# A node tile's steps in six places instead of eight, in a graph layer with a mixture of experts

## What is computed

```python
xn = layernorm(x)
# graph part: weighted sum over the edges of each node
n_emb = segment_sum(edge_weight[:, None] * xn[src], dst, 12500)
g = leaky(xn @ W1.T + b1 + (n_emb + n_emb * xn) @ W2.T + b2)
g = g / max(sqrt(sum(g * g)), 1e-12)
# mix part: linear attention; k and v are normalized per head, k.T @ v is a 32 x 32 table per head
ret = per_head(q(xn) @ (k(xn).T @ v(xn)) / 12500) + xn
m = gelu(ret @ w1 + b1) @ w2 + b2 + xn
x = x + g + m
# top-1 mixture of experts, 8 experts, each takes the first 1.25 * 12500 / 8 tokens
h = layernorm(x)
probs = softmax(h @ gate_w + gate_b); e = argmax(probs)
y = (relu(h @ w1[e] + b1[e]) @ w2[e] + b2[e]) * probs[e] * kept
return x + y
```

## Time and profile before

| What | Value |
|---|---|
| median of three runs | 2520.43 us |
| the profiled execution | 2522.2 us, its span 2520.3 us |
| mean granted clock of TensorE | 0.919 of full speed |
| busy: PE, DVE, ACT, POOL | 82%, 60%, 41%, 72% of the span |
| moved by DMA | 594.32 MB, mean 236 GB/s |
| POOL's last gather of edge rows | 2213.83 us |

### The profile page before, as it was taken

How to read it: one execution, slowest core, us unless ns; L and a number is a source line. 1 busy time by engine, 2 the same in 40 slices (tenths; PEclk the granted TensorE clock), 3 DMA queues, 4 the chain that set the end, 5 groups by cost and what they waited for, 6 DMA issues and landing times. The chain is left out here.

```text
span 2520.3 us, 42814 instructions
## 1 busy us (share of the span) xinstructions
PE 2056.2 (82%) x12889; PEld 1586.9 (63%) x12889; DVE 1514.9 (60%) x5328; ACT 1036.6 (41%) x2482; POOL 1810.3 (72%) x1888
## 2 busy tenths in 40 slices
PE   0049999994677777899989999998989899796898
PEld 0015656662455556776767777777777777685787
DVE  6676555554457786787646656666556556555233
ACT  4662333331344454553434433443444444342333
POOL 7777777777777777777777777777777777723654
PEclk9968999997788888999989999999999999897999
DMA  9845666664566667777777776777888888775896
GB/s 338 310 142 169 175 173 175 174 174 131 153 197 193 193 198 259 231 240 231 237 229 248 239 229 221 241 236 237 320 280 306 300 316 285 247 260 221 330 349 248
DMA packets 279341, 594.32 MB, mean 236 GB/s; under 512 B 48437, under 2 KB 177214, under 8 KB 256863
## 3 DMA queue, kind: packets, MB, share of 16 engines
q0 software_dynamic: 93168, 256.28, 33.8%
q1 hardware_dynamic: 155553, 284.06, 32.6%
q10 hardware_dynamic: 30390, 51.21, 5.5%
HBM read 506.22 MB, written 87.99 MB: 236 GB/s over the span
## 5 line engine op out<-in xcount | busy, mean ns | idle before, releaser
L931 POOL DMA_INDIRECT rows_sb<-xn_scratch,src_sb x1517 | 1459.0, 962 | 464.2 <-issue 455.8
L1199 PE MATMUL bank<-acc 128*128 128x128 f32 (+1 forms) x2624 | 442.3, 322 | 15.0 <-issue 10.9
L1220 PE MATMUL bank<-acc 128*128 128x256 f32 x1680 | 413.1, 390 | 0.0
L1199 PEld LDWEIGHTS bank<-acc 128*128 128x128 f32 x2624 | 384.9, 204 | 40.8 <-issue 18.6
L1020 PE MATMUL bank<-rows_sb,s_sb 128*24 128x256 f32 x3082 | 225.7, 413 | 202.0 <-DMA rows_sb<-xn_scratch,src_sb 197.4
L1963 ACT ACTIVATE acc<-bank,acc 128x128 f32<-128x128 f32 (+1 forms) x656 | 212.0, 398 | 375.8 <-PE bank L1199 375.7
L1220 PEld LDWEIGHTS bank<-acc 128*128 128x128 f32 x1680 | 313.9, 194 | 49.7 <-issue 0.9
L1484 DVE TENSOR_TENSOR acc<-acc,bank 128x48 f32 x831 | 170.4, 205 | 273.7 <-PE bank L1030 160.4
L1020 PEld LDWEIGHTS bank<-rows_sb,s_sb 128*24 128x24 f32 x3082 | 84.9, 107 | 274.9 <-issue 232.5
L1884 ACT COPY sums<-bank 120x256 f32<-120x256 f32 x208 | 76.5, 368 | 347.2 <-PE bank L1020 347.2
L1915 ACT ACT_TABLE_LOAD x95 | 121.9, 1283 | 194.8 <-PE bank L1109 193.9
(11 more groups left out here) (263 smaller groups left out, 3649.9 us busy)
## 6 DMA issues: line engine op xcount, KB each, us to landing
acc<-ffn_first_in SPq DMA_DIRECT2D x82, 1028.0 KB
acc<-ffn_w_in SPq DMA_DIRECT2D x82, 1024.0 KB
arena<-xn_scratch SPq DMA_DIRECT2D x194, 128.0 KB, 3.2
h_scratch<-arena ACTq DMA_DIRECT2D x97, 256.0 KB
rows_sb<-xn_scratch,src_sb POOLq DMA_INDIRECT x1517
xnt_scratch<-arena SPq DMA_DIRECT2D x97, 128.0 KB, 2.3
arena<-xnt_scratch SPq DMA_DIRECT2D x97, 128.0 KB
arena<-x_in SPq DMA_DIRECT2D x97, 128.0 KB
```

Source lines behind the costliest of these rows:

```text
L931: pool.indirect_dma_start(out=chunk_row(c), out_offset=None, in_=xn_d, in_offset=bass.IndirectOffsetOnAxis(ap=src_sb[:, c:c + 1], axis=0)) ...
L1199: m = pe.matmul(bank[:, i * tokens:(i + 1) * tokens], w1_sb[k % 2][:, h, f * P:(f + 1) * P], xt[:, k % 2, h, 0:tokens], start=h == 0, stop ...
L1220: m = pe.matmul(bank[:, i * D:(i + 1) * D], hid[:, f, i * P:(i + 1) * P], w2_sb[k % 2][:, f, :], start=False, stop=f == FC - 1 and i == 0)
```

## The change

A table now says how many places behind the entry a step comes. Steps 2 and 3 share the second place, steps 4 and 5 the third, 6 the fourth, 7 the fifth, and the logits come in the sixth. So that a place can hold both, ACT does square and root among its "early" steps, in this order, ahead of the ticks. SP loads a tile's rows one place earlier. Batches and units of the planner follow, two places sooner each; wanted_at is written another way, so that units 56 to 59 stay at place 208. There are 256 places instead of 258, and 55 units with 78 tiles are kept instead of 54 with 77. The last tile's slots are computed in place 215 instead of 217. The number of scatters of kept tiles per unit behind that is worked out from the numbers of places and comes to four instead of three.

```diff
 
 
 
-        KV_TICKS, KV_PAIRS, C_STEPS = T + 5, 43 + RAW_PAIRS, 9
+        KV_TICKS, KV_PAIRS = T + 5, 43 + RAW_PAIRS
+        STEP_AT = {0: 0, 1: 1, 2: 2, 3: 2, 4: 3, 5: 3, 6: 4, 7: 5}
+        LAP_AT, LOGIT_AT = 3, 6
         FIRST_KV = RAW_PAIRS + H + 1
         side = [[] for _ in range(PAIRS)]
 
...
         ends = dense + list(range(T - 3, dense[-1] + RT - 1, -RT))[::-1] + [T]
         routes = [range(a, b) for a, b in zip([0] + ends, ends) if a < b]
         assert T > 3 and all(len(v) <= RB for v in routes)
-        chosen_at = [enters[v[-1]] + C_STEPS - 1 for v in routes]
+        chosen_at = [enters[v[-1]] + LOGIT_AT for v in routes]
         rank_at = [p + (1 if p >= PAIRS else 2) for p in chosen_at]
         build_at, slots_at = [], []
         for b, tiles in enumerate(routes):
...
             return found if at_end else early_steps(p) + found
 
         def early_steps(p):
-            found = [("logit", t) for t, e in enumerate(enters) if e + 8 == p]
+            found = [("logit", t) for t, e in enumerate(enters) if e + LOGIT_AT == p]
             for b in range(len(routes)):
                 if chosen_at[b] + 1 == p:
                     found.append(("sums", b))
...
 
 
         PE_PLACE, PE_EXPERT, PE_TURN = 10.0, 3.3, 0.9
-        PE_STEP = {1: 1.2, 3: 3.0, 7: 0.5, 8: 0.7}
+        PE_STEP = {STEP_AT[1]: 1.2, STEP_AT[3]: 3.0, STEP_AT[7]: 0.5, LOGIT_AT: 0.7}
         e_ticks = [(k, j) for k in range(K + 1) for j in range(1, ticks(k) + 1)]
         first_tick = [n for n, (k, j) in enumerate(e_ticks) if j == 1]
         last_tick = [first_tick[k] + ticks(k) - 1 for k in range(K)]
         e_place, time, p = [], 0.0, FIRST_C
-        wanted_at = [slots_at[b] + (4 if slots_at[b] + 4 < PAIRS else 2) for b in batch_of]
+        wanted_at = [min(slots_at[b] + 4, max(slots_at[b] + 2, PAIRS)) for b in batch_of]
         for k, j in e_ticks:
             cost = PE_EXPERT + PE_TURN * (j == 1)
             if j == 1 and k < K:
...
             return psum[(2, 3, 1)[t % KV_BANKS]]
 
         def c_steps(p, order):
-            return [(enters.index(p - s), s) for s in order if p - s in enters]
+            return [(enters.index(p - STEP_AT[s]), s) for s in order if p - STEP_AT[s] in enters]
 
         def first_of(t):
             return max(v[0] for v in routes if v[0] <= t)
...
                         for part in range(2):
                             sp.dma_start(b2_raw[part * NE:(part + 1) * NE, :], ffn_b2).then_inc(w2_ld[0], 16)
                     elif kind == "early":
-                        for t, s in c_steps(k, (2, 0, 3)):
+                        for t, s in c_steps(k, (1, 0)):
                             if s == 0:
                                 load_turned(t)
-                            elif s == 2:
+                            else:
                                 load_rows(t)
-                            elif t + LAP_TILES < T:
-                                load_acc(t + LAP_TILES)
+                        if k - LAP_AT in enters and enters.index(k - LAP_AT) + LAP_TILES < T:
+                            load_acc(enters.index(k - LAP_AT) + LAP_TILES)
                 for k in w1_at[p]:
                     load_first(k)
                 for k in w2_at[p]:
...
                                    ).then_inc(kv_rooted, 1)
 
             def logit_group(t):
-                return groups_to(enters[t] + 8)
+                return groups_to(enters[t] + LOGIT_AT)
 
             def c_step(t, s):
                 r, par = rows(t), t % 2
...
                     for t, s in kv_steps(k, (3, 2, 1)):
                         kv_step(t, s)
                 elif kind == "early":
-                    for t, s in c_steps(k, (7,)):
+                    for t, s in c_steps(k, (7, 4, 5)):
                         c_step(t, s)
                     for b in range(len(routes)):
                         if chosen_at[b] + 1 == k:
...
                             act.activation(tmp[:, 0:len(routes[b]), :], lg[:, 0:len(routes[b]), :], ACT.Exp
                                            ).then_inc(r_exp, 1)
                 elif kind == "late":
-                    for t, s in c_steps(k, (4, 1)):
+                    for t, s in c_steps(k, (1,)):
                         c_step(t, s)
                 elif kind == "unit":
                     unit_tick(k)
 
             for p in range(PLACES):
-                for t, s in c_steps(p, (6, 5)):
+                for t, s in c_steps(p, (6,)):
                     c_step(t, s)
                 if p < PAIRS:
                     copy_pair(p)
```

## The result

The change makes the kernel slower, by less than half a per cent: a median of 2530.79 us (11 runs, 2528.54 to 2541.77) against 2522.18 us (11 runs, 2516.91 to 2527.71), ratio 1.0045 with a 95% interval of 1.0033 to 1.0057. The forecast was 2514.4 us, in a range of 2501 to 2526.

A forecast was written before the change was run, and what follows sets the result against it. POOL's gathers were taken to bound the kernel up to 2214 us. The stall's -10 us and the last units' +4 us gave -6 us on a 2520.3 us span, 2514.4 us as a median, in a range of 2501 to 2526.

The forecast's parts named there:

- What bounds the kernel: Up to 2214 us POOL's gather issue, about 10.1 us a place; savings count only behind POOL's last gather.
- third rival: Edge pairs: second product waits for DVE's neighbour sum, PE becomes the bound, about 2560 us; chance 0.10 with lesser mishaps.
- POOL's end: Last row gather 3.8 us later, last pair's turn at 2230 to 2233.4, place 210 about 1.5 us sooner.
- so the 3.8 us are paid out of PE's lateness: Last pair: three token gathers delay the last rows 3.8 us, hidden because PE came late to them before.
- The stall: Place 210 to unit 60's turn: that turn comes at 2297.3 against 2307.01, 10 us sooner, bounds 4 to 14.
- One wait of about 6 us on DVE: Head of place 211: one PE wait replaces those of 6.67 and 4.70 us.
- Unit 60 to 64: Stretch between these units' turns: same steps and units in the same order, shifted, so 0 change.
- a gain of 1 or 2 us from the clock: Unit 60 to 64: a shorter stall may leave more ticks at the higher clock; left to the range.
- The last units: Unit 64 to the end: four back scatters a unit, 2.75 MB more in 120 us, cost 4 us.
- second rival: Last units: transfers eat the gain, load queue's waits on scatters grow beyond 13.7 us, about 2520 us; chance 0.20.

The follow-up runs named there:

- the second experiment: Changed kernel with all four token gathers of units 56 to 59 behind the last gather of edge rows: 2523.64 us, ratio 1.0002 to before.
- the first trace: First profiled execution of the changed kernel, unaltered, the slowest of its eleven runs: 2541.77 us, span 2539.6 us.
- the fourth and the seventh experiment: Changed kernel, kept-tile loads asked for two places later: 2524.24 us; the same plus token gathers behind the last edge rows and three scatters a unit: 2519.01 us.
- the second traces: Changed kernel and kernel before, each run once more unaltered: 2531.58 and 2523.55 us, spans 2529.4 and 2521.8 us.
- the fourth experiment: Changed kernel, four scatters a unit, each load of kept tiles asked for two places later: 2524.24 us, ratio 1.0009 to before.

## Why the prediction was wrong

**What bounds the kernel: right.** POOL sets the pace up to the last gather, and what counts lies behind it. The third rival (PE becomes the bound of the pairs) did not come.

**POOL's end: wrong.** The step "so the 3.8 us are paid out of PE's lateness" failed. PE did come on time, as the prediction said, and just therefore met rows that were not there: 3.8 us of issue, then 8.1 us from the last gather's start to the use of its rows instead of the 4.2 of the second experiment (2212.57 to 2216.74), then products at half speed. The turn of the last pair was put at 2230 to 2233.4; it came at 2234.49 and 2243.69, and relative to the last gather 6 to 7 us later than worked out. The experiment prices the order of the gathers at about 11 us. Most of that is a gain that did not come: against the kernel before, the last pair's turn is only 0.3 to 1.5 us later behind the last gather, besides the 3.8 us of issue, where the prediction had it 1.5 us sooner in all. The prediction set the gathers' issue against a lateness and never asked when the rows land behind them. Whether the token gathers or the weights next to them held the rows up stays open.

**The stall: right.** From the last pair's turn to unit 60's turn 65.3 us were worked out; 66.0 and 66.7 came. That is not luck, as the parts agree too: in the first trace 27.8 us to the counts, 16.2 to the logit, 12.5 to the slots (2300.23) and 9.5 to unit 60's turn, where 26, 17.2, 12.0 and 10.1 were worked out. One wait of about 6 us on DVE was forecast, and 5.20 us came, ahead of the logit and not of the rank product. Taking the clean-up out of the chain gave 3.6 us for the 2.6 of the sum.

**Unit 60 to 64: mis-sized.** "The same steps, shifted: 0" came as 2.5 to 2.9 us more, at a granted clock of 0.85 where before it was 0.91 (2307 to 2348 us), with the same units. PE's busy time accounts for all of it (35.4 instead of 32.5 us in both pairs of traces). What the prediction left to the range as a gain of 1 or 2 us from the clock was a loss; why the clock was lower here stays open.

**The last units: wrong.** The term of 4 us measured 10 to 14. Bytes and POOL's issues were counted, and both would have been free, as the fourth and the seventh experiment show. What failed was the step from a wait in a queue to its price: the 13.7 us of SP's waits were in the earlier trace rows, and the second rival had them grow, but nothing was worked out for what stands behind the waiting load, nor for the lower clock at which PE goes on behind its waits.

In sum, from the second traces: last gather +0.8 (3.8 of issue hidden in the scatter of that row), last pair +1.5, stall -6.9, unit 60 to 64 +2.5, last units +9.7, together 7.6 us, as the spans differ (2529.4 against 2521.8) and near the 8.6 of the medians.

## What to carry to other kernels

Before a step moves nearer to another, list what the planner works out from the number of places (here a rounded-up count of scatters and the order of gathers), since these side effects were larger than the gain. A wait on a shared queue is free until the transfer behind it is the one that is needed next: price the transfer behind it, not the wait. And an engine that arrives earlier at its input gains nothing if the input itself comes later: look at what is asked for ahead of the input and next to it.

## What the runs showed of the hardware

A wait can cost more than its length: behind 7.34 us without work PE's granted clock was 0.72 in the next 13 us, and products of one shape took 1.91 us instead of 1.03. In the last stretch, PE's waits ahead of the first layer grew by 8.0 us, and another 7.4 us came as busy time at a lower clock (0.90 instead of 0.96). A transfer rate of 380 GB/s stood for 120 us in the fourth experiment, with gathers, scatters and weight loads together. The edge part of the same kernel, with the same instructions, took 2023.0 and 2033.0 us from first to last gather in two executions, which is what a change of this size has to be seen against.
